# A state-space block on one core: TensorE's sums for the first half of the next chunk's decays, moved to the head of its slot

## The reference

```python
zxbcdt = x @ W_in                       # z, xBC, dt
xBC = silu(causal_conv4(xBC) + conv_b)  # x_ssm, B, C
dt  = softplus(dt + dt_bias); dA = exp(dt * -exp(A_log))
s   = s * dA_t + dt_t * x_t * B_t       # one state per head, over all tokens
y_t = s C_t + D * x_t
y   = rms_norm(y * silu(z)) * norm_weight; out = x + y @ W_out
```

## Time and profile before

| | us |
|---|---|
| median of 3 runs | 1308.08 |
| the three runs | 1305.57, 1308.08, 1311.21 |
| the profiled execution: its own time | 1312.65 |
| its span, first to last instruction | 1310.9 |
| busy in the span: PE, DVE, POOL, ACT | 1062.4, 809.1, 655.7, 618.4 |

### The profile page before, as it was taken

How to read it: one execution, slowest core, us unless ns; L and a number is a source line. 1 busy time by engine, 2 the same in 40 slices (tenths; PEclk the granted TensorE clock), 3 DMA queues, 4 the chain that set the end, 5 groups by cost and what they waited for, 6 DMA issues and landing times. The chain is left out here.

```text
span 1310.9 us, 21923 instructions
## 1 busy us (share of the span) xinstructions
PE 1062.4 (81%) x6532; PEld 883.3 (67%) x6532; DVE 809.1 (62%) x1611; ACT 618.4 (47%) x1494; POOL 655.7 (50%) x593
## 2 busy tenths in 40 slices
PE   3747999999916788999999999989747999999900
PEld 3646999999914566766666666657536999999800
DVE  6974444444437898698989897875383444444434
ACT  1333555555513565556565656564333555555400
POOL 6913555555421465556565655567505555555300
PEclk9998999999966888788988888899868999999955
DMA  6861222222232111111111100000062222222178
GB/s 230 267 273 49 78 77 77 78 77 78 58 109 73 49 37 41 37 45 35 47 41 42 41 25 17 17 17 25 29 257 65 77 77 78 77 77 76 53 243 275
DMA packets 73242, 112.20 MB, mean 86 GB/s; under 512 B 10664, under 2 KB 60336, under 8 KB 71856
## 3 DMA queue, kind: packets, MB, share of 16 engines
q1 hardware_dynamic: 47888, 58.77, 13.2%
q0 software_dynamic: 13824, 37.77, 8.8%
q10 hardware_dynamic: 11424, 14.30, 3.2%
HBM read 66.76 MB, written 44.04 MB: 85 GB/s over the span
## 5 line engine op out<-in xcount | busy, mean ns | idle before, releaser
L399 POOL DMA_INDIRECT ys_d<-xs,row_of x144 | 142.0, 986 | 195.3 <-DVE xs L779 189.5
L768 DVE TENSOR_TENSOR xl<-pT,xh 128x256 fp32r<-128x256 f32 x144 | 61.1, 424 | 223.9 <-ACT xh L476 223.9
L394 POOL DMA_INDIRECT xs<-xn_d,token_of x144 | 139.8, 971 | 114.4 <-DVE token_of L753 71.2
L463 ACT ACTIVATE hs<-pH 128x512 f32<-128x512 f32 x144 | 86.0, 597 | 233.8 <-PE pH L581 233.8
L773 DVE TENSOR_TENSOR h2l<-hs,h2h 128x512 fp32r<-128x512 f32 x144 | 99.8, 693 | 78.0 <-ACT h2h L471 77.8
L1548 DVE SCALAR_TENSOR_TENSOR acc<-raw,cwh,acc 128x512 f32<-128x512 f32 x104 | 120.9, 1208 | 2.2 <-POOL acc L1075 1.2
L1171 ACT ACTIVATE ex<-bank,dts 128x128 f32<-128x128 f32 x256 | 72.5, 366 | 98.9 <-PE bank L1316 98.9
L601 PE MATMUL pY<-w2h,h2h 128*128 x576 | 102.8, 300 | 0.5 <-DVE h2l L773 0.3
L1060 POOL TENSOR_TENSOR yv<-yv,sz 128x512 f32<-128x512 f32 x32 | 48.0, 1501 | 95.8 <-DVE yv L1598 95.8
L581 PE MATMUL pH<-w1h,xh 128*128 x288 | 92.7, 404 | 1.8 <-DVE xl L768 1.1
L581 PE MATMUL pH<-w1l,xh 128*128 x288 | 92.7, 404 | 0.0
(11 more groups left out here) (248 smaller groups left out, 2668.8 us busy)
## 6 DMA issues: line engine op xcount, KB each, us to landing
m_yg<-ys_d SPq DMA_DIRECT2D x64, 128.0 KB, 2.1
xs<-ys_d SPq DMA_DIRECT2D x16, 512.0 KB, 6.0
wst<-in_L_ffn_w_dram ACTq DMA_DIRECT2D x8, 512.0 KB, 4.7
xs<-in_L_attn_x_dram SPq DMA_DIRECT2D x8, 512.0 KB, 6.6
hs<-in_L_ffn_w_dram ACTq DMA_DIRECT2D x8, 512.0 KB, 5.0
xn_d<-xs SPq DMA_DIRECT2D x8, 512.0 KB, 3.2
lo_d<-w1l SPq DMA_DIRECT2D x1, 4096.0 KB, 11.8
lo_d<-w2l SPq DMA_DIRECT2D x1, 4096.0 KB, 21.3
```

What stands on the lines that cost most here:

```text
L394: pool.indirect_dma_start(out=xg[:, t % NX, :], out_offset=None, in_=xn_d, in_offset=bass.IndirectOffsetOnAxis(ap=token_of[:, t:t + 1], ax ...
L399: pool.indirect_dma_start(out=ys_d, out_offset=bass.IndirectOffsetOnAxis(ap=row_of[:, t:t + 1], axis=0), in_=y[:, t % NX, :], in_offset=No ...
L463: act.activation(r[:, u, :], pH[u][:, :], ACT.Relu).then_inc(relu_done.sem, 1)
```

## The change

In PE's list of every slot the call of `sums(s + 1, 0)` goes from behind `out_product(s - 1)` to the head of the slot, ahead of `from_state(s)`. Its waits go with it. No instruction is added or taken away, and no other engine's list changes.

```diff
             for s in SLOTS:
                 first, late = blocks(s, PROJECTED)[:1], blocks(s, PROJECTED)[1:]
+                if live(s + 1):
+                    sums(s + 1, 0)
                 if live(s):
                     from_state(s)
                 if s == 2 - LEAD:
@@
                 if live(s - 1):
                     out_product(s - 1)
-                if live(s + 1):
-                    sums(s + 1, 0)
                 if live(s):
                     within(s)
                     to_state(s)
```

## The result

| | before | after |
|---|---|---|
| median, on the same chip | 1307.05 us (6 runs) | 1319.36 us (6 runs, 1316.62 to 1326.16) |
| ratio | | 1.0095 [1.0072, 1.0118] |
| profiled execution / its span | 1312.65 / 1310.9 us | 1319.51 / 1317.8 us |
| granted clock over the span | 0.897 | 0.892 |

The kernel is slower by some 12 us. The forecast was 1305 within 1298 to 1315: wrong sign, and outside its range.

What follows compares the result with a forecast made beforehand. The prediction took PE and DVE, handing each slot's end to each other, as the bound. Its terms, 2.7 - 2.3 - 3.65 = -3.2 us, about -3, on 1308.1 gave 1305, within 1298 to 1315.

Steps and rivals of the forecast that it cites:

- what one `sums` costs: On PE, 0.45 us for sums at the head, 0.85 freed behind an output product at low clock; total work unchanged.
- -2.3 - 3.65 = -5.95: Forecast gains in us for the odd slots: 2.3 in slots 1, 9, 17 and like, 3.65 in slots 3, 7, 11 and like.
- sign of being wrong by the clock: Over the whole run: the prediction is wrong by the clock if the sum of PE's low-clock stretches differs.
- The clock stood among the rivals: Work ahead of PE's stall shortens it and spares low-clock stretches in four of seven groups: 7 us more gain, 1298; chance 0.14.
- Slots 0 modulo 4: `from_state` reaches DVE's `scale_state` 0.45 us later in six slots: a loss of 2.7 us.
- Slots 1 modulo 4: PE's stall before `project_dt` covers the sums; in slots 9, 21 and 25 `within` starts earlier: a gain of 2.3 us together.
- Slots 2 modulo 4: Output product and residual come 0.45 us later, but DVE's 0.48 wait for `within` absorbs it: no change.
- Slots 3 modulo 4: PE's stall covers the sums and `within` comes 0.6 to 0.85 us earlier, cut short by DVE: a gain of 3.65 us together.
- POOL shut out: DVE keeps POOL's `gate_y` waiting, 4.0 us per event; three more events make 1317; chance 0.14.
- ACT as the bound: Earlier exponentials let ACT's list run 0.75 us earlier in some 16 slots: 12 us gain, 1296; chance 0.06.
- the four kinds: Slots grouped by number modulo 4; their bounds were said to put the change between +3 and -6 us, 1302 to 1311.
- The 0.64 for no change: Chance that the whole kernel's time stays within 0.5%, 6.5 us: neither below 1301.5 nor above 1314.6.

Runs made afterwards that it cites:

- Experiment 3: The kernel after, with the same five products made once more between output product and `within` in odd slots, into a free bank: 1309.47 us, ratio 1.0012.
- experiment 2: The kernel before, with the sums moved to the head in odd slots only: 1318.41 us, ratio 1.0062.
- experiment 5: The kernel after, unchanged, profiled and run once more: 1318.43 us, ratio 1.0071.
- kernel 8: The kernel before, with unread products in odd slots, eight ahead of `project_dt` and three ahead of the turning of x: 1292.78 us, ratio 0.9901.
- kernel 4: The kernel before, with eight unread products of 512 columns ahead of `project_dt` in odd slots: 1300.80 us, ratio 0.9942.
- kernel 6: The kernel after, with six unread products of 512 columns ahead of `project_dt` in odd slots: 1311.59 us, ratio 1.0034.
- kernels 4 and 7: The second of these is the kernel before with the sums directly behind `from_state` in every slot: 1325.14 us, ratio 1.0134.

## Why the prediction was wrong

**The step that failed** is in what one `sums` costs: "PE's total work per slot stays the same; what counts is on which side of a wait it lies." Everything behind it was summed at the clock that each slot had in the trace of before. But the five products between the output product and `within` were not neutral work. PE came out of its stall at 1.2 GHz, and in slots 9 and 13 of before it was back at 2.4 after 6.8 and 3.4 us. With `within` directly behind the output product it stayed down for 13.7 us there and in slots 3 and 21. Experiment 3 shows this: the same products put back there, into a bank nobody reads, return 10 of 12 us; experiment 2 shows that it lies in the odd slots, experiment 5 that it repeats. The odd slots had -2.3 - 3.65 = -5.95 in the sum; they measured +14.8, and the 30.8 us more at 1.2 GHz in them are up to 15.4 of it. The prediction's own sign of being wrong by the clock, a changed sum of low stretches, is met: 99.0 and 116.1 us.

**The clock stood among the rivals in one direction only.** I asked whether work in front of the stall would spare low stretches, gave that 0.14 at 1298, and never asked what would become of the stretch behind it. The earlier trace rows had the material: a product of 3.76 us, then the sum, then `within`. The other end of that question, a low stretch longer by 7 to 10 us in four of 15 odd slots at 3.0 to 5.9 us each, is the 16.4 of the result. What sets these four apart from the other eleven no run shows. The section on HAM oscillation in the Trainium skill (TensorE: Matmul & The Clock Gate) has idle gaps of PE bring the clock down, and this trace agrees as far as the drop goes (1.91 us of stall, then 3.76 for the product). It speaks of gaps only; here PE had a product in work through all 13.70 us of the stretch at 1.2 GHz.

**Slots 0 modulo 4: right.** `scale_state` waits 0.54 for `from_state` in slot 12 where it had taken it as it came. Slots 16 and 17 together went from 31.56 to 32.00, +0.44 for a forecast of 0.45.

**Slots 1 modulo 4: the mechanism as forecast, the price reversed.** In slot 9 `within` starts right behind the output product: 0.85 was to be regained, and the slot lost 3.0, since `within` took 3.53 instead of 2.35, `to_state` 1.97 instead of 1.07, and what follows was slow too. The stalls ahead of `project_dt` were to shrink from 2.07 to some 1.6. In slots 9, 13, 17 and 21 they took 1.91 to 1.93, since DVE came later too; in slots 3 modulo 4 from 7 to 23 they shrank as forecast, from 2.31 to 1.86 or 1.87.

**Slots 2 modulo 4: right where the clock allows the comparison.** Slot 18 takes 13.02 in both, with a residual wait of 2.68 where some 2.6 was forecast (it was 1.95 in that slot before). In slot 14 the clock was up in after (1.00 for 0.87 in the earlier trace rows), and the slot is 1.65 shorter for that reason.

**Slots 3 modulo 4: right in sign, less than half in size.** Slot 15 gave 0.37 for a forecast of 0.35, and DVE's `add_within` no longer waits, as it did in the earlier trace rows; slot 19 gave 0.4 for 0.5. But slots 7, 23 and 27, whose low time is 6.8 us in both profiles as well, gave 0.1, 0.1 and 0.2 for 0.5, 0.6 and 0.8. These five together gave 1.2 where 2.75 was forecast. Slots 3 and 11 lost 5.9 and 1.1 in the profile, with 10.3 and 3.4 us more at 1.2 GHz.

**POOL shut out: right in kind, nearly nothing in size.** One event went (slot 4) and one came (slot 24), so the number didn't grow, and the rival's price of 4.0 was 0.7 in slots 24 and 25. That its 1317 lies near the measured 1319 is luck: the loss came another way.

**ACT as the bound: refuted.** Its wait fell from 98.9 to 0.2 and nothing got faster. In slots 16 to 19, at the same clock, some 98.9 / 32 = 3.1 us a slot less of this wait moved the end by 0.04; ACT waited for DVE's moments instead. In kernel 8 that wait was still 69.7, and it is the fastest.

**The range.** The bounds named for the four kinds don't add up to +3 and -6: they make at least 6 x 0.88 = +5.3 on one side and -2.3 - 6 = -8.3 on the other. The measured +12.3 lies outside these too.

**The chances.** At a fixed clock the terms were small, as forecast, and of the right sign (+0.45 and -0.5 for slots 16 to 19, +0.44 and -0.4 measured), though the gain of slots 3 modulo 4 was put too high. The 0.64 for no change took the clock's placing for noise around zero, and only 0.14 for slower, all of it POOL's, left no room for a loss through the clock.

## What to carry to other kernels

- A wait that is large in the list and lies on an engine with time to spare buys nothing: 98.9 us of it went, and the kernel became 12 us slower.
- Before moving work on PE, look at its clock at the old place. If PE comes out of a stall at 1.2 GHz, what stands directly behind can decide how long it stays there (in four of 15 odd slots here), and a product that needs nothing may be worth more there than at the head. The price is that of the whole stretch behind, not of the moved products.
- Where PE waits for another engine and its clock falls for it, try products that nobody reads, into a free bank, short enough to end before the wait does. Eleven a slot in the odd slots were worth 14 us here (1306.6 to 1292.8).

## What the runs showed of the hardware

- PE can stay at 1.2 GHz for 13.7 us with a product in work all the time (595.60 to 609.30 in after). It came in that same length in slots 3, 9, 13 and 21, in the repetition in 5, 9, 13 and 21, and with the sums behind `from_state` in 3, 5, 21 and 22. The old order is no sure guard against it: kernel 4 has 13.7 us from slot 12 into 13, and before 10.2 from slot 4 into 5, both in slots with POOL's event.
- More work made the kernel faster: 8 + 3 products of 512 columns in each odd slot took the low clock in the block from 99.0 to 17.1 us in the profiles, and the time down by 1%.
- POOL's `gate_y` mostly takes 1.27, 1.57 or 1.66 us, and now and then some 5.6. In slot 24 it was 5.63 in all nine profiles whose sums were made early there, with DVE's `new_state` 0.66 behind the start of `add_within`; in the six others it was 1.27, with 1.00 between the two. These two, in the kernel after:
```profile
854.46 0.67 DVE L1598 TENSOR_TENSOR yv<-yv,bank 128x512 f32<-128x512 f32 x1
855.12 0.68 DVE L1606 TENSOR_TENSOR S<-S,bank 64x512 f32<-64x512 f32 x1
```
  A pause on DVE doesn't decide it alone, though. In slots 0, 4, 8, 12, 16 and 20 the two starts lie 0.60 or 0.61 apart in 84 cases over all profiles, so without a pause, and POOL's `gate_y` starts 0.81 behind `add_within` in each; it took 1.56 to 1.59 in 80 of them and 5.56 to 5.58 in four (slot 4 of before, slot 8 of kernel 6, slot 12 of kernels 4 and 7). In the long case DVE's convolution steps are 0.73 or 0.74 long and POOL waits for all six; in the short one DVE's first four steps take 1.52 to 1.73. What chooses between the two no run tells. The Trainium skill (SBUF — State Buffer, section Who interferes with whom) calls the shared pair of ports an exclusive lock, and says where it speaks of DVE's two-port modes that whoever issues first gets it for the whole instruction; slot 24 agrees that POOL can be kept out, but it is kept out through several of DVE's instructions in a row.
